# MLP phase of a one-core token-mixing, attention and expert kernel: second product in token order, rows normalised first, two pieces of the next first product drawn forward

## What is computed

```python
x = x + attn
h2 = _ln(x, g2, beta2)
x = x + (jax.nn.gelu(h2 @ w1 + b1, approximate=False) @ w2 + b2)
...
h = h + _L0_ffn_ref(_layernorm(h, axis=-1), ...)
# in _L0_ffn_ref:
full_logits = x @ gate_w.T          # 8 dynamic experts + 1 fixed
... sparse mixer, top-k by rank, running counts against a capacity ...
y_sh = jnp.einsum('tfi,fhi->tfh', jax.nn.silu(gs) * us, sh_down_w)
```

## Time and profile before

| | us |
|---|---|
| median of 3 runs | 2683.14 |
| lowest and highest | 2682.89, 2688.43 |
| the profiled execution | 2680.65 |
| its span, first to last instruction | 2678.9 |
| first and last `ob` of the MLP phase | 1712.4, 2470.7 |
| stores of `ob` 0 and 13 issued | 1714.04, 2382.6 |
| one step in the middle | 51.04 |

### The profile page before, as it was taken

One profiled execution on the slowest core, in us unless ns is written; L12 is line 12 of the kernel. 1 busy time (PEld: TensorE's weight loads), 2 busy tenths in 40 slices (PEclk: granted clock), 3 DMA queues, 4 the chain that ended last, 5 costly groups with the idle time before them and its releaser, 6 DMA issues. The chain is left out here.

```text
span 2678.9 us, 61218 instructions
## 1 busy us (share of the span) xinstructions
PE 2370.8 (88%) x22832; PEld 1728.2 (65%) x22832; DVE 1851.4 (69%) x4046; ACT 1533.9 (57%) x2859; POOL 1566.1 (58%) x1546
## 2 busy tenths in 40 slices
PE   3799999999999999999999957998998999995664
PEld 3588788888888888888888743444444444443553
DVE  3577777777777777777777742777877778775442
ACT  3566666666666666666666635555555655552232
POOL 1465656656565665656565532556656666666566
PEclk8999999999999999999999977999999999998888
DMA  4111111212111111111110020211211211100675
GB/s 150 44 62 62 43 60 62 66 37 66 62 41 62 41 41 41 45 37 41 42 40 26 14 82 25 70 48 60 80 52 57 79 49 41 46 21 16 151 138 71
DMA packets 115061, 152.21 MB, mean 57 GB/s; under 512 B 16537, under 2 KB 75917, under 8 KB 114768
## 3 DMA queue, kind: packets, MB, share of 16 engines
q1 hardware_dynamic: 88880, 124.46, 14.3%
q0 software_dynamic: 23808, 21.74, 4.6%
q10 hardware_dynamic: 2080, 2.10, 0.2%
HBM read 81.71 MB, written 90.96 MB: 64 GB/s over the span
## 5 line engine op out<-in xcount | busy, mean ns | idle before, releaser
L952 POOL TENSOR_TENSOR qkl<-fz,qkh 128x512 f16<-128x512 f32 x256 | 307.6, 1202 | 305.5 <-DVE qkh L849 305.5
L1817 POOL DMA_INDIRECT slot_dram<-xt,slot_u x256 | 258.5, 1010 | 74.5 <-issue 74.4
L521 PE MATMUL pF<-nh,qk_h 128*128 128x256 f16 x1024 | 281.2, 275 | 5.7 <-DVE nl L836 4.4
L523 PE MATMUL pF<-nl,qk_h 128*128 128x256 f16 x1024 | 280.6, 274 | 0.0
L522 PE MATMUL pF<-nh,qk_l 128*128 128x256 f16 x1024 | 280.6, 274 | 0.0
L964 POOL TENSOR_TENSOR ol<-on,oh 128x256 f16<-128x256 f32 x256 | 171.8, 671 | 153.3 <-ACT oh L786 153.3
L971 POOL TENSOR_TENSOR kvl<-kvacc,kvh 128x260 f16<-128x260 f32 x192 | 150.3, 783 | 108.1 <-ACT kvh L794 108.1
L763 ACT ACTIVATE sh<-sm 128x512 f16<-128x512 f32 x256 | 159.3, 622 | 84.9 <-DVE sm L872 84.9
L1797 POOL TENSOR_TENSOR al<-az,ah 128x512 f16<-128x512 f32 x64 | 78.9, 1232 | 204.3 <-DVE ah L1586 204.3
L740 ACT ACTIVATE rz<-pF 128x512 f32<-128x512 f32 x256 | 150.7, 589 | 81.9 <-PE pF L523 77.2
L846 DVE SCALAR_TENSOR_TENSOR fz<-pF,ez 128x512 f32<-128x512 f32 x256 | 175.3, 685 | 29.6 <-ACT ez L746 27.4
(11 more groups left out here) (313 smaller groups left out, 8565.7 us busy)
## 6 DMA issues: line engine op xcount, KB each, us to landing
xs<-in_x SPq DMA_DIRECT2D x128, 256.0 KB, 2.6
slot_dram<-blank SPq DMA_DIRECT2D x8, 1360.0 KB, 6.0
xg<-slot_dram SPq DMA_DIRECT2D x40, 272.0 KB, 3.2
h_dram<-hT SPq DMA_DIRECT2D x32, 256.0 KB, 2.1
x_dram<-x SPq DMA_DIRECT2D x32, 256.0 KB, 2.1
at_dram<-at SPq DMA_DIRECT2D x32, 256.0 KB, 2.2
x0b<-x_dram SPq DMA_DIRECT2D x16, 512.0 KB, 3.9
atb<-at_dram SPq DMA_DIRECT2D x16, 512.0 KB, 4.9
```

Source lines behind the costliest of these rows:

```text
L521: pe.matmul(out, wh, mh, start=first, stop=False, skip_group_check=True)
L523: return pe.matmul(out, wh, ml, start=False, stop=last, skip_group_check=True)
L952: nc.gpsimd.tensor_tensor(qkl[:, pair:pair + 2, cols], fz[:, n % 2, :, :], qkh[:, pair:pair + 2, cols], ALU.subtract).then_inc(fl_ready, 1)
L1817: nc.gpsimd.indirect_dma_start(io["slot_dram"], bass.IndirectOffsetOnAxis(slot_u[:, c, k:k + 1], 0), xt[:, i % 2, c, :], None, bounds_chec ...
```

## The change

`w2` now puts the tokens on the partitions: per piece, four chunks of 128 tokens with three 256-column matmuls each (`gh`, `gl` are the weights, `w2_h`, `w2_l` move). The residual goes into the same banks first, as eight full-precision 128x128 matmuls of `hx` against `ident_w`, the identity times 64. `hp`, `mean3`, `xc3`, `sq3`, `var3` and `turn_sums` are gone. ACT copies `pY` to `ht` (two copies); DVE takes mean and variance per token with `bn_stats` and `bn_aggr`; ACT makes `rs3` on 128x4 values; DVE writes `xn` in token order (four `tensor_scalar`). ACT (`cast3`) and POOL (`low3`) write its halves into `xt`, now three buffers instead of two, and the same 16 transposes (`turn_rows`, in two halves through a new bank `pX`) turn rows into features `xf`, which ACT copies (`copy_rows`) for `logits` and the next step's `gate_up`. All links behind `counts` (`rest`) now stand inside `w2`, ahead of the statistics. `down` is cut into four, and the first two pieces of the next `w1` (`w1_ahead`) stand before its last part.

```diff
                 s["mask"](i - 1)
-                s["w2"](i, range(7))
+                s["w2"](i, range(5))
                 if before:
                     s["counts"](i - 1)
-                s["w2"](i, range(7, FT))
+                    s["exp2"](i - 1)
+                    s["rest"](i - 1)
+                s["w2"](i, range(5, FT))
+                s["sums3"](i)
+                s["rstd3"](i)
+                s["norm3"](i)
                 if after:
                     s["var2"](i + 1)
-                if after:
                     s["scale2"](i + 1)
                 if before:
                     s["gate_up"](i - 1, after, (0,))
-                s["mean3"](i, before)
+                s["cast3"](i)
+                if before:
+                    s["gate_up"](i - 1, after, (1,))
                 if after:
                     s["shift2"](i + 1)
+                s["low3"](i)
                 if before:
-                    s["gate_up"](i - 1, after, (1, 2))
-                s["var3"](i)
+                    s["gate_up"](i - 1, after, (2,))
+                s["turn_rows"](i, 0)
                 if before:
                     s["gate_up"](i - 1, after, (3,))
-                s["rstd3"](i)
+                s["copy_rows"](i, 0)
+                s["rows_ahead"](i)
                 if before:
-                    s["down"](i - 1)
-                s["turn_rows"](i, before)
+                    s["down"](i - 1, (0,))
+                s["turn_rows"](i, 1)
+                s["copy_rows"](i, 1)
+                if before:
+                    s["down"](i - 1, (1,))
                 s["logits"](i)
-                s["turn_sums"](i)
+                if before:
+                    s["down"](i - 1, (2,))
+                if after:
+                    s["w1_ahead"](i + 1)
+                if before:
+                    s["down"](i - 1, (3,))
...
             def w2(i, js):
...
+                    for c in range(CH):
+                        toks = slice(c * P, (c + 1) * P)
+                        for t in range(DT):
+                            at = c // 2 * D + t * P
+                            mm = pe.matmul(pY[c % 2][:, at:at + P], hx[:, t, toks], ident_w[:, :], start=c < 2 and t == 0,
+                                           stop=False, skip_group_check=True)
...
-                    for m in range(DT):
-                        cols = slice(m * P, (m + 1) * P)
-                        mm = three(pY[m][:, :], w2_h[:, j, cols], w2_l[:, j, cols], gh[:, j, :], gl[:, j, :],
-                                   j == 0, j == FT - 1)
+                    for c in range(CH):
+                        toks = slice(c * P, (c + 1) * P)
+                        mm = three(pY[c % 2][:, c // 2 * D:(c // 2 + 1) * D], gh[:, j, toks], gl[:, j, toks],
+                                   w2_h[:, j, :], w2_l[:, j, :], False, j == FT - 1)
...
+            def turn_rows(i, half):
+                pe.wait_ge(xnh_ready, count(i, 2, half + 1))
+                pe.wait_ge(xnl_ready, count(i, 2, half + 1))
...
+            def sums3(i):
+                act.wait_ge(w2_done, count(i, 1, 1))
...
+                for b in range(2):
+                    nc.scalar.activation(ht[:, i % 2, b:CH:2, :], pY[b][:, :].rearrange("p (c n) -> p c n", c=2), ACT.Copy,
+                                         scale=1 / W2_SCALE).then_inc(ht_ready, 1)
```

More of the change, by code:

```diff
@@ L996 @@
 ROW = 272
+XT = 3
+COUNTS = 64
 def mlp_phase(nc, io, w1_w, w2_w, mlp_loaded, ew):
@@ L1207, in run @@
             s["counts"](SEQS - 1)
+            s["exp2"](SEQS - 1)
+            s["rest"](SEQS - 1)
             s["gate_up"](SEQS - 1, None, range(ST))
-            s["down"](SEQS - 1)
+            s["down"](SEQS - 1, range(ST))
         def at_start(i):
@@ L1399, in counts, with nothing @@
                 mm.then_inc(cum_done, 1)
-            def nothing(i):
+            def nothing(i, *rest):
                 pass
-            run(pe, dict(mean2=mean2, var2=var2, w1=w1, w2=w2, mean3=mean3, gate_up=gate_up, var3=var3, down=down,
-                         centre2=nothing, scale2=nothing, shift2=nothing, mask=nothing,
-                         rstd3=nothing, logits=logits, turn_rows=turn_rows, turn_sums=turn_sums,
-                         counts=counts))
+            run(pe, dict(mean2=mean2, var2=var2, w1=w1, w2=w2, gate_up=gate_up, down=down,
+                         centre2=nothing, scale2=nothing, shift2=nothing, mask=nothing, sums3=nothing,
+                         rstd3=nothing, norm3=nothing, low3=nothing, rows_ahead=nothing, logits=logits,
+                         rest=nothing, exp2=nothing, turn_rows=turn_rows, cast3=nothing, copy_rows=nothing,
+                          w1_ahead=w1_ahead, counts=counts))
         @block.scalar
@@ L1496, in turn_sums, with low3 @@
-            def turn_sums(i):
-                for half in range(2):
-                    act.wait_ge(ht_done, count(i, 2, half + 1))
-                    if not at_start(i):
-                        act.wait_ge(ob_ready, count(i, CH, 0))
-                    nc.scalar.activation(ht[:, 2 * half:2 * half + 2, :],
-                                         pA[half][:, :].rearrange("p (c n) -> p c n", c=2), ACT.Copy).then_inc(ht_ready, 1)
-            def counts(i):
-                exp_ln_tables(nc, act)
+            def low3(i):
+                if i < SEQS - 1:
+                    residual(i + 1)
@@ L1510, in nothing @@
                 pass
-            run(act, dict(mean2=mean2, centre2=centre2, var2=var2, scale2=nothing, shift2=shift2, mask=nothing, w1=w1, w2=nothing, mean3=mean3, gate_up=gate_up, var3=nothing,
-                          rstd3=rstd3, down=nothing, logits=logits, turn_rows=turn_rows, turn_sums=turn_sums,
-                          counts=counts))
+            run(act, dict(mean2=mean2, centre2=centre2, var2=var2, scale2=nothing, shift2=shift2, mask=nothing, w1=w1,
+                          w2=nothing, sums3=sums3, rstd3=rstd3, norm3=nothing, cast3=cast3, low3=low3, rows_ahead=nothing,
+                          gate_up=gate_up, down=nothing, logits=logits, turn_rows=nothing, copy_rows=copy_rows,
+                          counts=nothing, w1_ahead=nothing, rest=nothing, exp2=exp2))
             act.wait_ge(ew.w_in[0], 16)
@@ L1856, in mean2 @@
                     rows(i)
-            run(gp, dict(mean2=mean2, centre2=nothing, var2=var2, scale2=nothing, shift2=nothing, mask=nothing, w1=w1, w2=w2, mean3=mean3, gate_up=gate_up, var3=nothing,
-                         rstd3=rstd3, down=down, logits=nothing, turn_rows=nothing, turn_sums=nothing, counts=counts))
-            gp.wait_ge(rows_sent, 16 * CH * TOP * SEQS)
+            run(gp, dict(mean2=mean2, centre2=nothing, var2=var2, scale2=nothing, shift2=nothing, mask=nothing, w1=w1,
+                         w2=w2, sums3=nothing, rstd3=nothing, norm3=nothing, low3=low3, rows_ahead=rows_ahead,
+                         gate_up=gate_up, down=down, logits=nothing, turn_rows=nothing, copy_rows=nothing, cast3=nothing,
+                         w1_ahead=nothing, counts=counts, rest=nothing, exp2=nothing))
+            for i in range(SEQS - XT, SEQS):
+                sent(gp, i)
 ROUTE_STEPS = 51
```

335 lines of the change are left out of this document (172 added, 163 removed).

## The result

The changed kernel takes **2658.52 us** (2657.18 to 2661.64, 4 runs) against 2685.61 us (2682.89 to 2688.43, 4 runs) for the kernel before, beside it on the same chip: ratio 0.9904, 95% interval 0.9889 to 0.9918. It is faster by 27 us, inside the range of 2616 to 2662, but 22 us above the forecast of 2636: 27 of the 47 us came. The profiled execution took 2658.3 us, its span is 2656.6.

What follows compares the result with a forecast made beforehand. PE was taken to set the step, with gaps from the chain through DVE, ACT and POOL. Savings 35 + 5.3 + 5 + 2 = 47 us gave a 2633.5 us profiled execution, 2636 as median; range 2616 to 2662.

Steps and rivals of the forecast that it cites:

- longer chain: Rival: links behind `counts` and statistics stretched by sends, logarithm and `turn_rows` 2.5 us later a step; 2668 us, chance 0.16.
- PE's work: Middle step: 4.8 us of products removed, `hx` adds 2.0 and recut `w2` 0.12; net 2.7 us less.
- The chain to `turn_rows`: From T, end of the `counts` products, through links, statistics, logarithm, `gate_up`, `al` and `low3`: `turn_rows` at T+17.8.
- The rest of the step: PE work from `turn_rows` through `counts`, 30.3 us in all; with 17.8 makes 48.1, raised to a 48.35 us step.
- the gaps stay as large as they were: PE's idle gaps over a middle step would not shrink or grow; the gain is nearly all of the PE work saved.
- the thirteen steps: Intervals from first to fourteenth `ob` store: 13 steps at 2.7 us less, 35 us.
- The ends: Last two intervals: fifteenth `ob` another 2.6 us sooner (2.7 + 2.6), sixteenth about 5 us.
- The first step: Uncovered norm chain: two products and `turn_sums` less, statistics more, about 2 us saved.
- The shorter chain: Rival: statistics near the lower bound, no send in the way, T+9.75 becomes T+8.7; 1 us a step, 2622, chance 0.12.
- if even `low3` were in time: Further case of the shorter chain: PE alone sets a 44 us step, 2590 us.
- The slower case: Rival: `hx` loads and products at the head of `w2` not overlapped, 7.5 us instead of 2.0; 2707 us, chance 0.04.
- no effect: Rival: new order just moves the waits, for instance sends making the first `al` some 3 us late; 2683 us, chance 0.03.

Runs made afterwards that it cites:

- e10: Changed kernel with POOL making the rows' low halves ahead of the second `al`: 2605.5 us, ratio 0.9709 to the kernel before.
- e12: Changed kernel with eight useless 512-column matmuls in PE's row ahead of the wait before `turn_rows`, chip without the delay: 2640.2 us, ratio 0.9831 to the kernel before.
- e11: Changed kernel with the last four of eight POOL sends held until ACT has written the second product's rows: 2651.9 us, ratio 0.9877 to the kernel before.
- e9: Changed kernel with POOL's low halves ahead of the second `al` and the last four sends behind ACT's rows: 2603.1 us, ratio 0.9700 to the kernel before.
- e1: Changed kernel with the products of `counts` back behind seven pieces of `w2` instead of five: 2745.8 us, ratio 1.0064 to the kernel before.
- e6: The kernel before, run again without edit on a chip with the delay: 2735.7 us, ratio 1.0003.
- e5: The changed kernel, run again without edit on a chip with the delay: 2689.3 us, ratio 0.9826 to the kernel before.
- e3: Changed kernel with eight useless 512-column matmuls ahead of the wait before `turn_rows`, chip with the delay: 2680.9 us, ratio 0.9827 to the kernel before.
- e4: Changed kernel with the residual's eight full-precision products done twice, the first time into an overwritten bank: 2727.1 us, ratio 1.0007 to the kernel before.

## Why the prediction was half right

The range of 2616 to 2662 was drawn up to 2662 for a longer chain, which did not come. Two things that were not in it, a fall of the clock and a wait at `counts`, brought the time to 2658.5. That it lies inside is luck; the mechanism of the step up to `turn_rows` is not.

**PE's work: right.** 47.09 - 2.7 is 44.4; an undisturbed step has 44.28. `hx` took 1.78 us instead of 2.0: its columns set the pace, the lower bound. The `w2` records are 0.109 apart, as forecast.

**The chain to `turn_rows`: right.** With T = 2038.95 in the step of the 2057 rows, the links end at T+6.2 (forecast 6.4), the statistics at T+8.0 (forecast 8.5; `bn_stats` took 0.41 and `bn_aggr` 0.18, nearly the values taken), `gate_up(1)` starts at T+9.1 (forecast 9.75) and `turn_rows` at T+17.6 (forecast 17.8). The gaps are 0.68, 0.52 and 2.50 where 1.5, 0.6 and 2.3 were forecast. Of the 0.65 us won early, 0.45 was lost again on POOL: the second `al` took 1.59 and the first low half 1.60 where I had 1.15 and 1.16. e10 confirms that `low3` behind the second `al` is what sets this end.

**The rest of the step: 1.2 us short.** I had 30.3; it is 31.5 (49.10 - 17.6). The failed step is "`counts` 0.4" in "in all 30.3": I let the products of `counts` start as soon as PE reached them. They were moved ahead by two pieces of `w2`, 2.6 us, and their mask comes from DVE's links, which were not moved. So a wait that was 0.36 us in seven steps, 0.59 and 0.73 in two and absent in four became 1.11 in each. The mask is late because four links before it lie beside sends and additions of POOL, two of them here:

```profile
2028.37 1.62 DVE L1703 TENSOR_SCALAR few<-few 128x32 f32<-128x32 f32 x1
...
2031.01 1.81 DVE L1705 TENSOR_TENSOR few<-few 128x32 f32<-128x32 f32 x1
```

So the undisturbed step is 49.10, not 48.35.

**The clock: the term that was missing.** I wrote "the gaps stay as large as they were". They did not: PE's idle time grew from 3.95 us a step (51.04 - 47.09) to 4.82 (49.10 - 44.28), most of it by the wait at `counts`, and the largest gap grew from 1.83 to 2.50. Behind it the clock fell in ten of thirteen steps. No term of the sum and no rival had this. I took the 1.00 of the one middle step in the earlier trace rows for all; three of the thirteen were at 0.97.

**The account of the thirteen steps.** Forecast 35.1 us less; the trace has 668.1 - 655.7 = 12.4. Of the 22.7 us that are missing, the clock took 10 x 1.67 = 16.7 and the longer undisturbed step 13 x 0.75 = 9.8, together 26.5. The other way goes 3.8: the steps of the kernel before were 4.6 above thirteen times 51.04, 3.0 of it in the two long ones, and those after are 0.7 above what the two kinds of step make. The first term has its experiments (e12, and e11 beside e9). The second has none that stands by itself. The wait at `counts` is read from the trace, and e1, which was to test it, was covered by the delay. e10 shows what the 2.5 us wait is worth: without it the step is 46.9.

**The ends.** The fifteenth store came 6.2 us sooner in its interval (forecast 5.3, from 46.90 where 47.33 was right) and the sixteenth 11.0 (forecast 5): what stood ahead of the last links was worth more than twice my figure. The first step was to save 2 us, and saved 0.1 (113.0 us from its first `mean2` to the store, against 113.1). The clock there is at its lower level for some 33 us instead of 31, which is about 0.9 of the missing 1.9; the rest is open. `var2` of that step after, and before:

```profile
1610.98 3.71 PE L1295 MATMUL pA<-sq,ones 128*128 128x512 f32 x4 [2.04 <-ACT sq L1453]
...
1606.73 1.98 PE L1266 MATMUL pA<-sq,ones 128*128 128x512 f32 x4 [2.04 <-ACT sq L1422]
```

The MLP phase as a whole began 4.3 us later than in the trace before, and 3.2 us more lie behind the last store; the code of those places is the same in both kernels, and what differs from execution to execution there was not pursued. The profiled executions add up: 4.1 - 12.4 - 6.2 - 11.0 + 3.2 = -22.3, from 2680.65 to 2658.3.

**The rivals.** The shorter chain came by 0.65 of its 1.05 us up to `gate_up(1)`, and gained 0.2 of it at `turn_rows`. Its "if even `low3` were in time" priced e10's edit at 2590, and some 2605 is what it gives, with all other waits still there. (The 2590 does not follow either: from a step of 48.35, one of 44 us is 13 x 4.35 less than 2636, 2579.) The longer chain did not come: the links end 0.2 us ahead of the forecast. Sends stretch single copies (0.43 for 0.17, 0.3 us a step in all, which the forecast had), not all of them for half a send. The Trainium skill's page "SBUF — State Buffer", section "Who interferes with whom", taken as a lock on every copy beside a send, is more than these rows show. The slower case, with `hx` not overlapped, is excluded by the records, 0.111 apart. So is no effect by sends that make the first `al` late: POOL stood idle for 7.05 us ahead of it.

## What to carry to other kernels

- Before pricing a reordering by work saved, list the idle gaps of TensorE it leaves by size, not by sum, and read the granted clock of every step, not of one. Here one gap grew by 0.67 us and cost 1.67 more in clock in most steps; useless products in it bought some 20 us, and another order on GpSimd, which removed the gap, some 50.
- A fall of the clock costs what the waits behind it do not take up: 1.67 us a step in the changed kernel, 0.28 in the kernel before, nothing in e6.
- When a product is moved forward, move the chain that feeds it, or count the wait that appears. And price what is drawn forward as cover by the wait that it covers: here, on a chip with the delay, there was none, and drawing it forward gained nothing.
- Run the kernel itself as a control on the chip of the variants. Without e5, e3 would have passed for a gain, and e1 for a measure of the chain.

## What the runs showed of the hardware

- A gap of 2.50 us (in a few steps 2.85) was followed by the lower clock, for about 3.4 us, in ten of thirteen steps of the result's trace, in eight of e11's, in one of e5's and, with more work on TensorE, in all thirteen of e4's; a gap of 1.83 us (once 2.43) in three of thirteen in the kernel before. With gaps of 0.8 (e12) or 0.28 us (e9, e10) at this place all thirteen steps were at 1.00.
- On two of the chips TensorE's signals in a certain stretch of each step reach the other engines 3 to 6 us late (e1, e5, e6), worth 3.0 us a step to the kernel before and 41 and 50 us in all on the two chips. The stretch coincides with GpSimd's row of sends; whether they cause it was not settled. By themselves they do not: the same row stands in the result's trace, where the `ht` copy starts 0.04 us behind its product.
- Statistics of 128x256 take 0.41 us and their aggregation 0.18 on VectorE; a full-precision 128x128 product with its own weights takes 0.22 us in a row of eight.
